# Checking the adjacency chunks on VectorE plane by plane in a two-layer graph kernel

## The chip, the cores and the metric

The kernel runs on 1 core of one Trainium2 chip. The metric is the device time of one execution in microseconds (us), as a median of runs.

## The reference

Two graph layers with a norm ahead of each, on 4096 nodes of 128 features; `adj` is 4096 x 4096 float32 (64 MiB), drawn as zeros and ones with few ones.

```
h = relu(layernorm(x))
Wh = h @ W0;  e = leaky_relu(Wh @ a[:128] + (Wh @ a[128:]).T, 0.2)
alpha = softmax(where((adj > 0) | eye, e, -9e15), axis=1)
x = x + alpha @ Wh
h = relu(layernorm(x))
msg = h @ W1 + B
weights = where(adj < 1, exp(-(1/adj - 1)**2 / 0.5), 0)
out = x + weights @ msg
```

For an `adj` that holds only zeros and ones the weights of the second layer are all zero. The kernel takes this short way, and has to make sure of it: every element of `adj` is checked while it passes, and only if one is neither zero nor one (or another limit is passed) does a general branch at the end compute everything anew. It is not taken with these inputs.

## The kernel before

The adjacency matrix comes in 32 chunks of 2 MiB. Chunk i is [128 partitions x 4096 elements]: four planes (HK = 4) of 1024 columns (CW), each plane another block of rows. It lies in a ring of six slots (`ring`, AR = 6). SP's queue issues `load_chunk(i)` for i from 6 on once chunk i-6 has been packed by TensorE, turned where a turn is due, and checked, by VectorE or by ScalarE (lines 357 to 368).

What happens to each chunk:
- TensorE's `pack(i)` (L538) adds eight rows of the matrix, as bits, into words in PSUM (two chunks a step, 16 steps, two chunks for each of 4 column blocks in each of 4 groups of rows).
- VectorE's `scan(step)` (L1022) takes the highest eight words of each segment (MAX8, L1032), `pick(n)` (L1035) the highest of all of a piece (5 pieces of steps), TensorE's `place(n)` (L608) and VectorE's `decode(n)` (L1141) turn them into node numbers (`index`, L1155); what doesn't fit in a lane goes through `pick_shared` (L1067) and `decode_shared` (L1101) into `shared_index` (L1123).
- GpSimd fetches the rows of `node_table` that the numbers name, with one indirect DMA for each 128 numbers (L470, 76 of them, in groups for each piece). Its loop waits in order for `index_set` and `shared_index_set`.
- VectorE's `weigh(g)` (L1167) makes weights of the rows and spreads them (L1189 to L1200, L1206, L1218), TensorE's `scatter(g)` (L673, L669) adds them up, VectorE's `epilogue(s)` (L1266) ends a group of 1024 rows.
- The first block of columns goes another way: TensorE's `turn_columns(i)` (L519, L534) transposes it and VectorE's `column(i)` (L1242, L1253 and L1263) weighs it. Chunks with part of the diagonal are cleaned (`clean_diagonal`, L1013, L1018; chunk 6 in place, `clear_diagonal`, L1006, L1010).
- The check: 19 chunks by ScalarE in two passes (L845, L848), 13 by VectorE (`DVE_CHECKED` = 0, 1, 2, 4, 6, 10, 11, 14, 18, 20, 23, 25, 27) in `check(i)` (L994). One instruction (L1002) compares (x >= 1) with x over all 4096 elements of a partition and adds the differences to `bad_v[:, n]`; its results elsewhere go to a place that nobody reads (`trash_v`, the memory of `summed`). Near the end `judge()` (L1306, L1320) takes the maximum over `bad_v`.

The order of work on VectorE is written out by hand: checks 0 and 1 at L1346, then a loop over i from 2 to 31 (L1396 to L1431) in which each i has its cleaning, its check, its decoding, column(i - 1), scan, pick, weigh and epilogue as tables at the top of the file give them (L110 to L126); the check of chunk 25 comes at i = 26 (`LATE_CHECK`). TensorE's order is that of L714 to L747: for each i pack, turn, place, scatter. All engines wait on semaphores; `checked_v` counts the checks of VectorE. ScalarE and GpSimd have their own loops (L890, L457).

Of the kernel before, what the change touches and what calls it, by code (L numbers as in the profile page):

```python
# [5 lines left out]
N, D, P = 4096, 128, 128  # L6
# [5 lines left out]
CW = N // CC  # L12
HK = 4
CHUNKS = SG * CC * 2
AR = 6
# [91 lines left out]
NVC, NAC = len(DVE_CHECKED), len(ACT_CHECKED)  # L107
# [21 lines left out]
def gnn_program(nc, x, adj, w0, a0, w1, b1, out):  # L129
    fp32, bf16, fp8, i32, u32 = (mybir.dt.float32, mybir.dt.bfloat16, mybir.dt.float8e4, mybir.dt.int32,  # L130
                                 mybir.dt.uint32)
    ALU, ACT, AX = mybir.AluOpType, mybir.ActivationFunctionType, mybir.AxisListType
# [10 lines left out]
    with ctx:  # L143
        def sb(name, shape, dt=fp32):
            return ctx.enter_context(nc.sbuf_tensor(name, shape, dt))

        def sem(name):
            return ctx.enter_context(nc.semaphore(name))

        ring = sb("adj_ring", [P, AR, HK * CW])  # L150
# [73 lines left out]
        shared_on = sb("shared_on", [P, 2, KB, KB, HK])  # L224
        edge_w = sb("edge_w", [P, GE, KB])
        full = sb("full", [P, len(PIECES), 3])
        bad_v = sb("bad_v", [P, NVC])
        signs = sb("signs", [P, NAC])
        sizes = sb("sizes", [P, NAC])
        excess = sb("excess", [P, NAC])  # L230
# [22 lines left out]
        trash_v = summed[:, :, :].bitcast(fp8).rearrange("p k n -> p (k n)")[:, 0:HK * CW]  # L253
# [34 lines left out]
        def acc_of(t):  # L288
# [17 lines left out]
        checked_v, signed, checked_a, diag_cleared, diag_clean, packed, scanned = (  # L306
            sem(n) for n in ("checked_v", "signed", "checked_a", "diag_cleared", "diag_clean", "packed", "scanned"))
# [6 lines left out]
            sem(n) for n in ("picked", "removed", "full_seen", "placed_set", "words_done", "decode_step", "index_set", "bits_set",  # L314
                             "table_stored"))
        gathered = [sem(f"gathered{g}") for g in range(RING_GROUPS)]
        weight_step, spread_set, scattered, acc_read, epilogue_step, finished, stored = (
            sem(n) for n in ("weight_step", "spread_set", "scattered", "acc_read", "epilogue_step", "finished",
                             "stored"))
# [625 lines left out]
        def _(dve):  # L945
# [48 lines left out]
            def check(i):  # L994
                n = DVE_CHECKED.index(i)
                dve.wait_ge(adj_ready[i % AR], (i // AR + 1) * 16)
                done = sum(1 for at in EPILOGUE_AT if at < i)
                if done:
                    dve.wait_ge(finished, done)
                if n:  # L1000
                    dve.wait_ge(checked_v, n)
                nc.vector.scalar_tensor_tensor(trash_v, ring[:, i % AR, :], 1.0, ring[:, i % AR, :],  # L1002
                                               ALU.is_ge, ALU.not_equal,
                                               accum_out=bad_v[:, n:n + 1], saturate=False).then_inc(checked_v, 1)

            def clear_diagonal(i):  # L1006
                dve.wait_ge(checked_v, DVE_CHECKED.index(i) + 1)
# [338 lines left out]
            for i in range(2):  # L1346
                check(i)
# [48 lines left out]
            for i in range(2, CHUNKS):  # L1396
                if i in CLEANED:
                    clean_diagonal(i)
                if i in DVE_CHECKED and i != LATE_CHECK:
                    check(i)  # L1400
# [17 lines left out]
                if i == LATE_CHECK + 1:  # L1418
                    check(LATE_CHECK)
# [119 lines left out]
```

## Time and profile before

| | before |
|---|---|
| median of 3 runs | 231.09 us (230.5 to 231.35) |
| the profiled execution | 230.85 us |
| its span | 229.0 us |
| mean granted TensorE clock | 0.88 |
| busy: DVE, ACT, PE, POOL | 195.2, 178.3, 153.4, 124.8 us |
| L1002, 13 instructions | 57.4 us, 4419 ns each |
| L470, gathers by index, 48 | 75.4 us, 1572 ns each |
| L470, gathers by shared index, 28 | 34.3 us, 1225 ns each |
| DMA | 76.95 MB, mean 336 GB/s |

PE is TensorE, PEld its weight loads, DVE VectorE, ACT ScalarE, POOL GpSimd, SP the engine that issues the loads. The table by stretches gives the busy time of each engine in each stretch, with the number of instructions, then the granted clock of TensorE as a share of 2.4 GHz, the busy share of the 16 DMA engines (rounding of packets can take it over 1) and what they moved. A row of the timeline is start, duration, engine, line, operation, tile written and tiles read, shapes and count; in brackets stands how long the engine had been idle before it and what released it. An indirect DMA's row on POOL is the making of its descriptors, not the transfer.

### The profile page before, as it was taken

What the parts mean: (1) busy time and instruction counts of PE and PEld (TensorE: products, weight loads), DVE (VectorE), ACT (ScalarE), POOL (GpSimd) and SP (SyncE); (2) the same over time, 40 slices, a digit from 0 to 9 for tenths busy, and PEclk for the clock granted to TensorE, in tenths of its full rate; (3) what the DMA queues carried; (4) which work ended last, traced back from release to release, by engine and by line L of the source; (5) the groups of instructions that cost most, each with busy time, mean ns of one, the idle gap of its engine ahead of it and who ended that gap; (6) DMA issues with size and microseconds to landing.
All of it is one profiled execution on the core that took longest, in us unless ns stands there. A gap on an engine that the chain in (4) does not pass through costs nothing.

```text
span 229.0 us, 3107 instructions
## 1 busy us (share of the span) xinstructions
PE 153.4 (67%) x893; PEld 102.3 (45%) x906; DVE 195.2 (85%) x595; ACT 178.3 (78%) x166; POOL 124.8 (55%) x130
## 2 busy tenths in 40 slices
PE   0286789930976956798299865975982697908450
PEld 0285565410455634465166522653750264508340
DVE  7975999908999999997799799689999996998584
ACT  0799983999399999989998879979393989992000
POOL 0198004000001788888759787783588782777600
PEclk9999999995697995999889997799799589785996
DMA  5999999999999999999999999999999994122002
GB/s 158 364 411 410 406 409 409 419 425 406 411 408 407 402 398 391 398 397 401 390 387 399 400 395 397 404 388 399 405 386 400 402 390 181 29 45 98 20 3 97
DMA packets 22388, 76.95 MB, mean 336 GB/s; under 512 B 2643, under 2 KB 3255, under 8 KB 22368
## 3 DMA queue, kind: packets, MB, share of 16 engines
q1 hardware_dynamic: 18624, 70.26, 78.4%
q0 software_dynamic: 3040, 5.34, 6.9%
q10 hardware_dynamic: 704, 1.12, 1.3%
q8 instruction: 9, 0.15, 0.3%
q14 instruction: 11, 0.09, 0.1%
HBM read 74.52 MB, written 4.28 MB: 344 GB/s over the span
## 4 chain that ended last, share of the span: by engine, by line
DMA 30%; DVE 27%; PE 19%; issue 12%; ACT 8%; POOLq 1%; POOL 1%; DVEq 0%; SPq 0%
DMA adj_ring<-in_adj 29%; PE bank L567 9%; DVE summed L1002 6%; ACT spread L814 5%; DVE hub_w L1235 3%; DVE cand L1032 2%; PE bank L669 2%; ACT whe L828 2%; ACT gathered_rows L820 1%; DVE spread L1218 1%; PE bank L554 1%; POOL gathered_rows L470 1%; POOLq L143 1%; DVE stats L979 1%; DMA gathered_rows<-node_table,shared_index 1%
## 5 line engine op out<-in xcount | busy, mean ns | idle before, releaser
L470 POOL DMA_INDIRECT gathered_rows<-node_table,index x48 | 75.4, 1572 | 46.3 <-DVE index L1155 32.9
L845 ACT ACTIVATE trash_a<-adj_ring,below_one 128x4096 fp8e4<-128x4096 f32 x19 | 70.5, 3708 | 11.4 <-DMA adj_ring<-in_adj 10.0
L567 PE MATMUL bank<-adj_ring,pack_w 128*128 128x512 bf16 (+3 forms) x257 | 72.5, 411 | 3.8 <-DMA adj_ring<-in_adj 3.0
L848 ACT ACTIVATE trash_a<-adj_ring 128x4096 fp8e4<-128x4096 f32 x19 | 68.7, 3617 | 0.6
L1002 DVE SCALAR_TENSOR_TENSOR summed<-adj_ring 128x4096 fp8e4<-128x4096 f32 x13 | 57.4, 4419 | 10.2 <-issue 6.6
L567 PEld LDWEIGHTS bank<-adj_ring,pack_w 128*128 128x128 bf16 x262 | 26.8, 106 | 34.9 <-issue 12.0
L470 POOL DMA_INDIRECT gathered_rows<-node_table,shared_index x28 | 34.3, 1225 | 8.5 <-issue 8.2
L669 PE MATMUL bank<-gathered_rows,spread 128*128 128x129 f32 x176 | 24.1, 295 | 7.4 <-DVE spread L1218 4.5
L669 PEld LDWEIGHTS bank<-gathered_rows,spread 128*128 128x128 f32 x176 | 22.7, 208 | 9.0 <-issue 8.9
L1032 DVE MAX8 cand<-bank 128x8 f32<-128x120 f32 (+25 forms) x82 | 23.3, 351 | 0.5 <-PE bank L567 0.5
L554 PE MATMUL bank<-codes,code_w 128*128 128x512 bf16 x24 | 11.0, 459 | 16.8 <-issue 14.9
L603 PE MATMUL bank<-whe,hub_w 128*128 128x129 f32 x64 | 10.6, 321 | 5.5 <-DVE hub_w L1239 5.4
L814 ACT ACTIVATE spread<-x_sb,shift,rstd 128x128 f32<-128x128 f32 x32 | 13.2, 498 | 0.0
L554 PEld LDWEIGHTS bank<-codes,code_w 128*128 128x128 bf16 x32 | 3.5, 109 | 20.5 <-issue 17.0
L603 PEld LDWEIGHTS bank<-whe,hub_w 128*128 128x128 f32 x64 | 9.3, 224 | 7.4 <-DVE hub_w L1239 7.2
L502 PE MATMUL bank<-w_sb,gathered_rows 128*128 128x130 f32 x64 | 10.4, 313 | 1.4 <-ACT whe L828 1.3
L490 PE MATMUL bank<-ident,spread 128*128 128x128 f32 x32 | 6.5, 338 | 6.8 <-ACT spread L814 6.8
L502 PEld LDWEIGHTS bank<-w_sb,gathered_rows 128*128 128x128 f32 x64 | 9.3, 223 | 2.6 <-ACT gathered_rows L820 2.3
L836 ACT ACTIVATE hub_mask<-bank 128x512 fp8e4<-128x512 f32 x8 | 4.3, 591 | 7.4 <-PE bank L515 7.4
L534 PE MATMUL bank<-ident_bf,adj_ring 128*128 128x128 bf16 x31 | 3.3, 231 | 9.8 <-DVE col_w L1263 6.2
L1235 DVE TENSOR_SCALAR hub_w<-r_hub,whe 128x128 f32<-128x128 f32 x32 | 8.9, 355 | 0.0
L663 PE MATMUL bank<-hub_whe,col_w 128*128 128x129 f32 x48 | 8.7, 357 | 0.0
(168 smaller groups left out, 228.1 us busy)
## 6 DMA issues: line engine op xcount, KB each, us to landing
adj_ring<-in_adj SPq DMA_DIRECT2D x32, 2048.0 KB, 23.3
node_table<-whe POOLq DMA_DIRECT2D x4, 532.0 KB, 10.9
x_sb<-in_x SPq DMA_DIRECT2D x8, 256.0 KB, 6.4
out<-outb ACTq DMA_DIRECT2D x2, 512.0 KB, 7.5
gathered_rows<-node_table,index POOLq DMA_INDIRECT x48, 5.9
out<-outb SPq DMA_DIRECT2D x1, 512.0 KB, 2.7
gathered_rows<-node_table,shared_index POOLq DMA_INDIRECT x28, 5.4
out<-outb SPq DMA_DIRECT2D x2, 192.0 KB, 2.3
```

What stands on the lines that cost most here:

```text
L470: pool.indirect_dma_start(out=rows[:, g % RING_GROUPS * GE + t, :], out_offset=None, in_=table, in_offset=bass.IndirectOffsetOnAxis(ap=row ...
L502: last = nc.tensor.matmul(bank[6 + half][:, b * (D + 2):(b + 1) * (D + 2)], hT[:, nb * P:(nb + 1) * P], w0_sb[:, :], start=(b == 0), stop= ...
L554: nc.tensor.matmul(to[:, :], code_w[:, 2 * c + half, :], codes[:, :], start=True, stop=False, skip_group_check=True)
L567: last = nc.tensor.matmul(to[:, lo:hi], pack_w[:, k, :], ring_hi[:, i % AR, row_at + lo:row_at + hi], start=False, stop=(k == KB - 1), ski ...
L603: last = nc.tensor.matmul(bank[7][:, 0:E1], hub_w[:, m % 2, b, :], whe[:, 4 * HUB_ORDER[m] + b, ONE:ONE + E1], start=(m + b == 0), stop=(m ...
L669: return nc.tensor.matmul(acc_of(t), spread[:, g % 2, t * KB:(t + 1) * KB, :], rows[:, g % RING_GROUPS * GE + turn, ONE:ONE + E1], start=F ...
L814: last = nc.scalar.activation(hn_block(b), x_sb[:, b, :], ACT.Identity, bias=shift[:, b:b + 1], scale=rstd[:, b:b + 1])
L845: nc.scalar.activation(trash_a[:, :], ring[:, i % AR, :], ACT.Sign, bias=below_one[:, :], scale=-1.0, accum_out=signs[:, n:n + 1], saturat ...
L848: nc.scalar.activation(trash_a[:, :], ring[:, i % AR, :], ACT.Abs, accum_out=sizes[:, n:n + 1], saturate=False).then_inc(checked_a, 1)
L1002: nc.vector.scalar_tensor_tensor(trash_v, ring[:, i % AR, :], 1.0, ring[:, i % AR, :], ALU.is_ge, ALU.not_equal, accum_out=bad_v[:, n:n + ...
L1032: last = nc.vector.max(cand[:, at * 8:(at + 1) * 8], word_bank(step, half)[:, lo:hi])
L1235: last = nc.vector.tensor_scalar(hub_w[:, m % 2, b, :], r_hub[:, :], whe[:, nb, QA:QA + 1], whe[:, nb, AA:AA + 1], ALU.mult, ALU.max)
```

## The change

`check(i)` issues four instructions, one for each plane of 1024 elements, in place of one over 4096. Each has its own column of `bad_v`, which grows from 13 to 52. All four write the first 1024 bytes of `trash_v`, so each waits for the one before it, on a new semaphore `plane_checked`; the last one counts `checked_v`, as the one instruction did. `judge` is unchanged and reduces the larger `bad_v`.

```diff
-        bad_v = sb("bad_v", [P, NVC])
+        bad_v = sb("bad_v", [P, NVC * HK])
...
+        plane_checked = sem("plane_checked")
...
                 if n:
                     dve.wait_ge(checked_v, n)
-                nc.vector.scalar_tensor_tensor(trash_v, ring[:, i % AR, :], 1.0, ring[:, i % AR, :],
-                                               ALU.is_ge, ALU.not_equal,
-                                               accum_out=bad_v[:, n:n + 1], saturate=False).then_inc(checked_v, 1)
+                for k in range(HK):
+                    plane = ring[:, i % AR, k * CW:(k + 1) * CW]
+                    if k:
+                        dve.wait_ge(plane_checked, n * (HK - 1) + k)
+                    nc.vector.scalar_tensor_tensor(trash_v[:, 0:CW], plane, 1.0, plane, ALU.is_ge, ALU.not_equal,
+                                                   accum_out=bad_v[:, n * HK + k:n * HK + k + 1], saturate=False).then_inc(
+                                                       checked_v if k == HK - 1 else plane_checked, 1)
```

## Rows read from the trace of the kernel before

**Rows 1.** The table by stretches: us, busy (x) PE, PEld, DVE, ACT, POOL, PEclk, DMA, GB/s.

```profile
10.00:20.00 10.00, 7.79 (x40) 7.02 (x40) 6.23 (x46) 10.00 (x30) 8.98 (x14) 1.00 1.03 414
...
180.00:186.00 6.00, 6.00 (x28) 3.38 (x27) 5.93 (x23) 5.31 (x5) 4.48 (x6) 0.63 1.02 394
...
191.00:193.00 2.00, 2.00 (x16) 1.01 (x14) 0.10 (x2) 1.91 (x3) 0.00 (x0) 1.00 0.38 147
```

**Rows 2.** Timeline of VectorE, its waits for transfers from 100 to 160 us.

```profile
110.08 0.23 DVE L1189 TENSOR_TENSOR edge_w<-r_slots,gathered_rows 128x64 f32<-128x64 f32 x1 [2.54 <-DMA gathered_rows<-node_table,index]
...
130.51 4.43 DVE L1002 SCALAR_TENSOR_TENSOR summed<-adj_ring 128x4096 fp8e4<-128x4096 f32 x1 [1.26 <-DMA adj_ring<-in_adj]
...
148.43 4.42 DVE L1002 SCALAR_TENSOR_TENSOR summed<-adj_ring 128x4096 fp8e4<-128x4096 f32 x1 [2.23 <-DMA adj_ring<-in_adj]
...
153.97 0.69 DVE L1018 TENSOR_TENSOR clean<-adj_ring,offdiag 128x512 bf16<-128x512 f32 x1 [1.11 <-DMA adj_ring<-in_adj]
```

**Rows 3.** Timeline of VectorE from 168 us.

```profile
168.11 4.42 DVE L1002 SCALAR_TENSOR_TENSOR summed<-adj_ring 128x4096 fp8e4<-128x4096 f32 x1
...
172.46 1.35 DVE L1032 MAX8 cand<-bank 128x8 f32<-128x376 f32 x3
173.73 4.43 DVE L1002 SCALAR_TENSOR_TENSOR summed<-adj_ring 128x4096 fp8e4<-128x4096 f32 x1
...
178.93 0.69 DVE L1263 TENSOR_TENSOR col_w<-col_w,bank 128x512 f32<-128x512 f32 x1
...
193.31 0.17 DVE L1155 SCALAR_TENSOR_TENSOR index<-words_i,empty_i 128x8 int32<-128x8 int32 x1
...
207.70 0.16 DVE L1123 TENSOR_TENSOR shared_index<-shared_column,shared_empty 128x4 int32<-128x4 int32 x1
```

**Rows 4.** Timeline of TensorE from 179 us.

```profile
179.68 0.61 PE L534 MATMUL bank<-ident_bf,adj_ring 128*128 128x128 bf16 x4 [6.23 <-DVE col_w L1263]
...
180.51 1.91 PE L567 MATMUL bank<-adj_ring,pack_w 128*128 128x512 bf16 x4
...
192.26 0.42 PE L622 MATMUL bank<-slots,own_lane 128*32 128x8 f32 x8
```

**Rows 5.** Timeline of GpSimd, its last 16 gathers.

```profile
194.24 0.99 POOL L470 DMA_INDIRECT gathered_rows<-node_table,index  x1 [4.15 <-DVE index L1155]
...
211.61 1.00 POOL L470 DMA_INDIRECT gathered_rows<-node_table,shared_index  x1 [0.30 <-issue]
```

**Rows 6.** Timeline of VectorE, checks of chunks 0, 1 and 6.

```profile
20.54 4.42 DVE L1002 SCALAR_TENSOR_TENSOR summed<-adj_ring 128x4096 fp8e4<-128x4096 f32 x1
...
25.07 4.43 DVE L1002 SCALAR_TENSOR_TENSOR summed<-adj_ring 128x4096 fp8e4<-128x4096 f32 x1
...
52.47 4.43 DVE L1002 SCALAR_TENSOR_TENSOR summed<-adj_ring 128x4096 fp8e4<-128x4096 f32 x1 [6.58 <-issue]
...
56.93 0.69 DVE L1010 TENSOR_TENSOR adj_ring<-adj_ring,offdiag 128x512 f32<-128x512 f32 x1
```

**Rows 7.** Timeline of VectorE, shorter instructions and the check of chunk 14.

```profile
99.19 1.23 DVE L1200 TENSOR_TENSOR spread<-edge_w,lane_of_p 128x1024 f32<-128x1024 f32 x1
100.33 4.42 DVE L1002 SCALAR_TENSOR_TENSOR summed<-adj_ring 128x4096 fp8e4<-128x4096 f32 x1
...
160.40 0.69 DVE L1018 TENSOR_TENSOR clean<-adj_ring,offdiag 128x512 bf16<-128x512 f32 x1
```

**Rows 8.** The answer on the tile adj_ring, its last line.

```profile
DMA to landing us min/median/max: 11.5/23.3/27.6
```

**Rows 9.** Timeline of GpSimd, gathers from 99 to 169 us.

```profile
99.68 1.61 POOL L470 DMA_INDIRECT gathered_rows<-node_table,index  x1 [0.30 <-issue]
...
148.04 0.99 POOL L470 DMA_INDIRECT gathered_rows<-node_table,shared_index  x1 [0.30 <-issue]
...
155.84 1.00 POOL L470 DMA_INDIRECT gathered_rows<-node_table,shared_index  x1 [0.30 <-issue]
...
168.79 4.61 POOL L470 DMA_INDIRECT gathered_rows<-node_table,index  x1 [0.31 <-issue]
```

## The prediction

> **What bounds the kernel now.** I read the table by stretches first. From 10 us to 186 us the DMA engines are busy for the whole time (a share of 1.02 or 1.03 in each of 18 stretches; the first and the last are shown) and move some 400 GB/s. At 191 us, when the last chunk of the adjacency matrix is nearly in, the share falls to 0.38 [rows 1]. So up to about 190 us no engine shortens the kernel by being quick: a chunk arrives when its bytes have been moved. VectorE (DVE) shows it: its checks of chunks 20 and 23 and the cleaning of chunk 24 start after waits for the DMA of 1.26, 2.23 and 1.11 us [rows 2].
>
> Then I read VectorE after the last of these waits, because from there nothing is given back. It cleans chunk 24 at 153.97 us [rows 2] and works without an idle time over 0.23 us to column(26) at 178.93, with the checks of chunk 25 (168.11) and chunk 27 (173.73) on the way [rows 3]. TensorE (PE) stands for 6.23 us until 179.68, released by that L1263, and from there works through packs 28, 29 and 30 without a pause to place(3) at 192.26 [rows 4]. VectorE makes the index of L1155 from it at 193.31 [rows 3], and GpSimd (POOL), idle for 4.15 us until then, issues its last 16 gathers from 194.24, one every 1.3 us or more, with no longer pause than 0.3 us; the last four start at 211.61 [rows 5]. They end at about 216.5, and VectorE's last weights and the epilogue follow.
>
> The chain of waits goes another way into the tail: through the load of chunk 31 and the shared index of L1123. I don't follow it. That index is ready at 207.86 [rows 3], but the first gather that needs it starts at 211.61, behind twelve others and with only its usual 0.30 us of idle time [rows 5]; that branch is over 3 us early. What sets the end is chunk 24, then VectorE to 179.6, TensorE to 193.0, VectorE to 193.5, GpSimd to 216.5.
>
> **The cost of one check.** An instruction of 4096 elements takes 4.42 us [rows 3]. L1018 with 512 elements takes 0.69 us and L1200 with 1024 takes 1.23 [rows 7], a slope of 0.54 / 512 = 1.05 ns an element; from L1200 to the check it is 3.19 / 3072 = 1.04. So a plane of 1024 takes 4.42 - 3072 x 0.00104 = 1.22 us, as L1200 does. From the start of a check to the start of what follows without a wait are 4.35 us (168.11 to 172.46) [rows 3], so the last plane costs 4.35 - 3.20 = 1.15. The three that are waited for cost more. Check 1, which waits for check 0, starts 4.53 us after it, and L1010, which also waits for its check, comes 4.46 us after it [rows 6]; less 3.20 that is 1.26 to 1.33. A check in four parts takes 3 x (1.26 to 1.33) + 1.15 = 4.93 to 5.14 us, that is 0.58 to 0.79 more. I take 0.70, nearer to check 1, which is the same kind of instruction behind its like. All 13 checks make VectorE 9.1 us busier.
>
> The Trainium skill ("VectorE: DVE Perf Modes", section "The DRAIN you can't avoid") says that a semaphore between two instructions costs nothing extra. By that the planes would be 1.15 us apart and a check would take 0.25 us more; rows 6, where the waiting instruction comes 0.11 and 0.18 us later than 4.35, don't agree, and the rows decide.
>
> **Which of the 13 count.** Checks 0, 1, 2 and 4 lie ahead of an idle time of 6.58 us before check 6 [rows 6]. They delay the first packs by some 1.2 us, while chunks are queued. Checks 6, 10, 11 and 14 lie ahead of the wait of 2.54 us for a gather at 110.08: 4 x 0.70 = 2.8 us, so 0.3 is left. Check 18 lies ahead of 1.26 us, check 20 ahead of 2.23, check 23 ahead of 1.11 [rows 2]; each covers the 0.70 before it, the first also the 0.3. What runs late in between are packs, and through them and the checks SP's next load_chunk. A chunk lands 11.5 us or more after its issue [rows 8] and 2 MB take 5.2 us at 400 GB/s, so at least 6 us of other transfers are ahead of it, and a load issued up to 2.8 us later lands no later. If that cover were gone it would be up to 0.70 at each. Two checks, 25 and 27, have no cover: 2 x 0.70 = 1.40 us (bounds 1.16 and 1.58) on the path to 179.68 and on to the index.
>
> **GpSimd.** A gather takes 1.00 us undisturbed. The one at 168.79, in the check of chunk 25, takes 4.61 and ends at 173.40, 0.87 us after the check (172.53). The one at 99.68 takes 1.61 and ends at 101.29, 0.87 after L1200 (100.42) [rows 3, 7, 9]. Eight of the 76 gathers, of 4.02 to 4.82 us, stand like this in eight checks, 3.3 us each over 1.00. What lets one go is the end of a single instruction: that of 99.68 got through although the check of 100.33 had already begun. So with planes a gather waits 1.2 us at most; by its beat of 1.3 us about two are held in a check, for 0.6 + 1.2 us. GpSimd gains 3.3 - 1.8 = 1.5 us a check, some 12 us. None of it reaches the end: it stands 4.15 us for the index before 194.24, and no check is left behind that. The Trainium skill says in "SBUF — State Buffer", section "Who interferes with whom", that a VectorE instruction with two SBUF inputs shuts out a GpSimd one that reads SBUF for the whole instruction; the trace agrees, with these 0.87 us.
>
> What earlier gathers cost is DMA time. Four start from 148.04 to 155.84 [rows 9], most of whose bytes move behind chunk 24. By the 4.5 us gained in checks 18, 20 and 23 one to four of them go ahead of it, each 128 x 133 x 4 bytes = 68 KB, 0.17 us at 400 GB/s. Chunk 24 lands 0 to 0.7 us later; I take 0.2, as of those that move forward part was ahead before.
>
> **The rest.** judge reduces 52 partial results in place of 13: 39 x 1.05 ns = 0.04 us, nothing even on the path. Nothing is added to SP's or ACT's queue.
>
> The sum on the profiled execution: 230.85 + 1.40 + 0.20 = 232.45 us. That execution (span 229.0 us, 1.85 around it) lies 0.24 under the median of the runs, so the forecast is 231.09 + 1.60 = **232.7 us**, 0.7% more. Its own range is 232.0 to 233.4 (both ends of the two terms: 1.16 and 2.28, the lower less 0.25 for the runs' scatter).
>
> **Rivals.** (1) The delay is partly covered by TensorE's clock. After its 6.23 us of standing TensorE runs at 1.2 GHz for a while: the granted clock is 0.63 from 180 to 186 us, and four matmuls of L567 take 1.91 us [rows 1, 4]. If the clock comes back at the same moment although TensorE starts 1.6 us later, half of that is made up: 231.9, or 231.8 with no shift of chunk 24. Nothing in one trace ties the return to TensorE's start, which is for it; it can as well fall the other way, which is against it.
> (2) The gathers count after all, and the kernel gets faster. The place is the wait of 2.54 us at 110.08 [rows 2]: gathers come there some 5 us earlier. If the loads behind it had been late because of it, 2.5 us come off, less 1.40 for the uncovered checks: 230.0. It decides only if the DMA has gaps before 190 us; shares of 1.02 and more [rows 1] speak against it.
> (3) Planes and gathers hold each other up. If a gather that has got in between two planes makes the next plane wait until it is done, it costs up to 0.87 us; two a check in checks 25 and 27 are 3.5 us: 236.2. The Trainium skill, same page and section, has it that issue order decides who blocks. Against it speaks the check at 100.33, which took 4.42 us like the others with a gather under way until 101.29 [rows 7, 9].
> (4) The planes cost less than rows 6 say: 0.25 us a check gives 231.09 + 0.5 + 0.2 = 231.8.
>
> **How the numbers follow.** Forecast 0.54; (1) 0.20; (4) 0.10; (2) 0.08; (3) 0.08. The low end, 231.0, takes in (1) and (4) with the scatter of the runs and no shift; the high end, 234.0, the upper bounds (233.4) and a weak form of (3), one gather in each check. What is left out is (2), most of (3) and small tails. A measurement of this kernel tells about 0.5%, 1.2 us here, from no change, so the line is at 232.25. (1), (4) and a little of the forecast's lower side lie under it: same 0.35, slower 0.57, faster 0.08.
>
> **What would show it.** Right: 52 instructions on VectorE of about 1.22 us, 1.26 to 1.33 apart within a check; no gather over 2.3 us in a check; the cleaning of chunk 24 at 154.0 to 154.7; TensorE's wait ahead of turn_columns(27) ending near 181.3; the index of piece 3 near 195; GpSimd's last gather ending near 218. Wrong: that index still at 193.5 (a cover that I missed); planes over 1.4 us apart (rival 3); planes 1.15 apart (4); DMA shares clearly under 1.0 before 190 us.

## The result and the profile after

| | before | after |
|---|---|---|
| median | 231.01 us (230.5 to 231.35, 4 runs) | 233.91 us (232.61 to 234.35, 4 runs) |
| the profiled execution, its span | 230.85, 229.0 us | 234.35, 232.1 us |
| mean granted TensorE clock | 0.88 | 0.852 |

The ratio is 1.0118, with a 95% interval of 1.0074 to 1.0163: the change costs 2.7 us (1.7 to 3.8), where 1.6 had been forecast. Line numbers of after: the check is L1007 (before L1002), `clean_diagonal` L1023, `index` L1160, `column` L1268, `shared_index` L1128, the gathers L471.

The page of after, its groups (busy us, mean ns of one | idle before them, and what ended it):

```profile
L471 POOL DMA_INDIRECT gathered_rows<-node_table,index x48 | 52.1, 1085 | 73.0 <-DVE index L1160 59.5
...
L1007 DVE SCALAR_TENSOR_TENSOR summed<-adj_ring 128x1024 fp8e4<-128x1024 f32 x52 | 63.8, 1227 | 8.6 <-issue 3.8
...
L471 POOL DMA_INDIRECT gathered_rows<-node_table,shared_index x28 | 32.2, 1150 | 8.5 <-issue 8.2
```

Thirteen checks of 4419 ns have become 52 planes of 1227 ns, 6.4 us more work on VectorE. The 76 gathers take 84.3 us in place of 109.7. GpSimd has gained 25.4 us, and the kernel is slower all the same: what GpSimd gained shows up as its idle time ahead of the index.

The timeline of VectorE after (start, duration, operation; in brackets the idle time before it and what released it), from the checks of chunks 20, 23, 25 and 27 to its last epilogue:

```profile
130.76 1.23 DVE L1007 SCALAR_TENSOR_TENSOR summed<-adj_ring 128x1024 fp8e4<-128x1024 f32 x1 [0.61 <-DMA adj_ring<-in_adj]
...
149.82 1.23 DVE L1007 SCALAR_TENSOR_TENSOR summed<-adj_ring 128x1024 fp8e4<-128x1024 f32 x1 [2.73 <-DMA adj_ring<-in_adj]
...
155.02 0.69 DVE L1023 TENSOR_TENSOR clean<-adj_ring,offdiag 128x512 bf16<-128x512 f32 x1 [0.16 <-DMA adj_ring<-in_adj]
...
168.98 1.22 DVE L1007 SCALAR_TENSOR_TENSOR summed<-adj_ring 128x1024 fp8e4<-128x1024 f32 x1
170.12 0.08 DVE L1007 DVE_READ_ACCUMULATOR summed<-adj_ring 128x1 f32 x1
170.24 1.23 DVE L1007 SCALAR_TENSOR_TENSOR summed<-adj_ring 128x1024 fp8e4<-128x1024 f32 x1
...
171.51 1.23 DVE L1007 SCALAR_TENSOR_TENSOR summed<-adj_ring 128x1024 fp8e4<-128x1024 f32 x1
...
172.78 1.23 DVE L1007 SCALAR_TENSOR_TENSOR summed<-adj_ring 128x1024 fp8e4<-128x1024 f32 x1
...
175.20 1.21 DVE L1007 SCALAR_TENSOR_TENSOR summed<-adj_ring 128x1024 fp8e4<-128x1024 f32 x1
...
180.98 0.69 DVE L1268 TENSOR_TENSOR col_w<-col_w,bank 128x512 f32<-128x512 f32 x1
...
195.63 0.17 DVE L1160 SCALAR_TENSOR_TENSOR index<-words_i,empty_i 128x8 int32<-128x8 int32 x1
...
229.21 0.61 DVE L1307 SCALAR_TENSOR_TENSOR outb<-summed,rden,x_sb 128x128 f32<-128x128 f32 x2
```

TensorE and GpSimd after, same columns:

```profile
181.73 0.61 PE L535 MATMUL bank<-ident_bf,adj_ring 128*128 128x128 bf16 x4 [8.48 <-DVE col_w L1268]
...
194.58 0.42 PE L623 MATMUL bank<-slots,own_lane 128*32 128x8 f32 x8
...
219.36 6.49 PE L670 MATMUL bank<-gathered_rows,spread 128*128 128x129 f32 x32 [3.44 <-DVE spread L1223]
```

```profile
169.66 1.41 POOL L471 DMA_INDIRECT gathered_rows<-node_table,index  x1 [0.30 <-issue]
171.37 1.00 POOL L471 DMA_INDIRECT gathered_rows<-node_table,index  x1 [0.30 <-issue]
172.68 1.00 POOL L471 DMA_INDIRECT gathered_rows<-node_table,index  x1 [0.30 <-issue]
...
196.57 1.00 POOL L471 DMA_INDIRECT gathered_rows<-node_table,index  x1 [11.46 <-DVE index L1160]
...
218.00 1.07 POOL L471 DMA_INDIRECT gathered_rows<-node_table,shared_index  x1 [0.30 <-issue]
```

Followed through, against the rows of before:
- The cleaning of chunk 24 is at 155.02, 1.05 later [rows 2]. Not all of this is the transfer of chunk 24. VectorE's check of chunk 23 already starts 1.39 us later, as chunk 23 lands (149.82 against 148.43), and takes 0.60 more; VectorE is free only at 154.86, 0.89 after the moment at which it started the cleaning before. The wait of 1.11 us ahead of the cleaning is down to 0.16.
- The check of chunk 25 starts 0.87 later, column(26) 2.05 later [rows 3]: the two checks between them brought 1.18, that is 0.59 each.
- TensorE's wait ends 2.05 later, place(3) is 2.32 later [rows 4], the index and the first gather 2.32 and 2.33 [rows 3, 5]. The last gather ends at 219.07 (218.00 + 1.07), 2.6 us later.
- VectorE's last epilogue ends at 229.82 (229.21 + 0.61); before it ended at 226.14: 3.7 later. About 1.1 us have been added behind the last gather. After that the end of the kernel gives 0.6 back; the span is 3.1 longer.

What was added behind the gathers comes with a lower clock of TensorE. Its last two scatters are one row of 6.49 us after, with no pause in it (above); before they were two rows:

```profile
216.58 2.02 PE L669 MATMUL bank<-gathered_rows,spread 128*128 128x129 f32 x16 [3.28 <-DVE spread L1218]
219.84 2.02 PE L669 MATMUL bank<-gathered_rows,spread 128*128 128x129 f32 x16 [1.23 <-DVE spread L1218]
```

The table by stretches (us, busy and count of PE, PEld, DVE, ACT, POOL, granted clock, DMA share, GB/s), first after, then before:

```profile
177.00:187.00 10.00, 5.27 (x17) 2.66 (x18) 9.83 (x27) 7.51 (x4) 6.28 (x7) 0.51 1.03 388
...
218.00:225.00 7.00, 5.64 (x26) 5.67 (x27) 4.29 (x21) 0.00 (x0) 1.07 (x1) 0.51 0.04 7
```

```profile
177.00:187.00 10.00, 7.32 (x34) 4.24 (x35) 9.79 (x31) 9.31 (x5) 8.01 (x7) 0.66 1.02 393
...
218.00:225.00 7.00, 2.63 (x22) 2.28 (x20) 6.62 (x28) 0.00 (x0) 0.00 (x0) 1.00 0.09 32
```

From 177 to 187 us the clock is at its lower level, 1.2 GHz, for longer than before, after a wait of TensorE of 8.48 us; from 218 to 225 us, where the last scatters run, it is at 1.2 in place of 2.4 GHz.

### The profile page after: what moved, and what is told of

It reads as the page before. It is cut to its first block, busy times and chain, and to the rows that moved or that the text cites. A ratio compares the mean times of both kernels' runs of the same rounds, so it can differ in the third digit from the quotient of the medians.

```text
span 232.1 us, 3198 instructions
## 1 busy us (share of the span) xinstructions
PE 157.6 (68%) x906; PEld 106.1 (46%) x906; DVE 202.4 (87%) x673; ACT 178.5 (77%) x166; POOL 100.6 (43%) x130
## 4 chain that ended last, share of the span: by engine, by line
DMA 28%; DVE 25%; ACT 21%; PE 12%; issue 11%; DVEq 0%; POOL 0%; SPq 0%; ACTq 0%; POOLq 0%
DMA adj_ring<-in_adj 26%; ACT trash_a L846 10%; DVE summed L1007 8%; ACT trash_a L849 7%; PE bank L568 5%; PE bank L670 4%; ACT spread L815 3%; DMA gathered_rows<-node_table,shared_index 2%; DVE spread L1223 1%; PE bank L555 1%; DVE cand L1037 1%; DVE stats L980 1%; PE bank L664 1%; DVE summed L1278 1%; DVE summed L1299 1%
## 5 line engine op out<-in xcount | busy, mean ns | idle before, releaser
L471 POOL DMA_INDIRECT gathered_rows<-node_table,index x48 | 52.1, 1085 | 73.0 <-DVE index L1160 59.5
L568 PE MATMUL bank<-adj_ring,pack_w 128*128 128x512 bf16 (+3 forms) x262 | 71.8, 404 | 0.6 <-DMA adj_ring<-in_adj 0.6
L1007 DVE SCALAR_TENSOR_TENSOR summed<-adj_ring 128x1024 fp8e4<-128x1024 f32 x52 | 63.8, 1227 | 8.6 <-issue 3.8
L568 PEld LDWEIGHTS bank<-adj_ring,pack_w 128*128 128x128 bf16 x262 | 26.6, 105 | 31.2 <-issue 9.6
L471 POOL DMA_INDIRECT gathered_rows<-node_table,shared_index x28 | 32.2, 1150 | 8.5 <-issue 8.2
L670 PE MATMUL bank<-gathered_rows,spread 128*128 128x129 f32 x176 | 26.2, 313 | 8.2 <-DVE spread L1211 3.7
L670 PEld LDWEIGHTS bank<-gathered_rows,spread 128*128 128x128 f32 x176 | 24.8, 225 | 9.6 <-issue 9.1
L555 PE MATMUL bank<-codes,code_w 128*128 128x512 bf16 x32 | 14.3, 447 | 14.2 <-issue 12.1
L535 PEld LDWEIGHTS bank<-ident_bf,adj_ring 128*128 128x128 bf16 x31 | 2.2, 106 | 18.5 <-DVE col_w L1268 10.2
```

The costliest lines, as they stand in the source:

```text
L471: pool.indirect_dma_start(out=rows[:, g % RING_GROUPS * GE + t, :], out_offset=None, in_=table, in_offset=bass.IndirectOffsetOnAxis(ap=row ...
L555: nc.tensor.matmul(to[:, :], code_w[:, 2 * c + half, :], codes[:, :], start=True, stop=False, skip_group_check=True)
L568: last = nc.tensor.matmul(to[:, lo:hi], pack_w[:, k, :], ring_hi[:, i % AR, row_at + lo:row_at + hi], start=False, stop=(k == KB - 1), ski ...
L670: return nc.tensor.matmul(acc_of(t), spread[:, g % 2, t * KB:(t + 1) * KB, :], rows[:, g % RING_GROUPS * GE + turn, ONE:ONE + E1], start=F ...
L1007: nc.vector.scalar_tensor_tensor(trash_v[:, 0:CW], plane, 1.0, plane, ALU.is_ge, ALU.not_equal, accum_out=bad_v[:, n * HK + k:n * HK + k + ...
```

## The experiments

One table first, since most verdicts are read from it: starts of the cleaning of chunk 24 (L1018), column(26) (L1263) and index 3 (L1155), and the end of the last gather, each from one profiled execution; then the ratio of the runs. Lines by before's numbers. "Planes" says which checks are split.

| kernel | planes | clean 24 | column(26) | index 3 | last gather ends | ratio (95%) |
|---|---|---|---|---|---|---|
| before | none | 153.97 | 178.93 | 193.31 | 216.5 | 1 |
| e0_before_again | none | 154.48 | 179.67 | 194.19 | 216.9 | one run, 232.15 us |
| after | all 13 | 155.02 | 180.98 | 195.63 | 219.1 | 1.0118 (1.0074 to 1.0163) |
| e1_two_whole | all but 25, 27 | 155.75 | 180.54 | 195.17 | 218.1 | 1.0014 (0.9992 to 1.0035) |
| e2_only_two | 25, 27 | 153.74 | 180.10 | 194.52 | 216.9 | 1.0031 (1.0 to 1.0061) |
| e3_no_wait | all 13, unchained | 156.07 | 181.31 | 196.03 | 219.3 | 1.006 (1.0027 to 1.0092) |
| e6_pad | none, 11 lengthened | 153.87 | 178.65 | 193.17 | 216.2 | 1.0029 (1.0003 to 1.0056) |
| e7_half_gathers | none | 152.84 | 178.76 | 193.14 | 215.9 | one run, 230.42 us |
| e8_split_18_20_23 | 18, 20, 23 | 155.06 | 179.85 | 194.46 | 217.7 | one run, 232.84 us |

**The kernel before once more**, for how far two profiles of one kernel lie apart.

> The kernel before, once more, for a second trace. If the later cleaning of chunk 24 after the change (155.02 us against 153.97) is an effect of the change, it stands at 153.7 to 154.3 here. If it is scatter between executions, it can lie anywhere from 153.5 to 155. Time 230.5 to 231.4 us.

Chunk 24 is cleaned 0.5 us later and index 3 comes 0.9 later than in the first profile, with not a line changed. So shifts of half a us at chunk 24 are no evidence by themselves. The executions here with whole checks ahead of chunk 24 and all gathers (these two, e2, e6 and the five kernels with check 27 moved, below: nine in all) have it at 153.6 to 154.5.

**The covered checks split, the two uncovered ones whole**, and the reverse.

```diff
+PARTS = [1 if i in (25, 27) else HK for i in DVE_CHECKED]     # e1_two_whole
+PARTS = [HK if i in (25, 27) else 1 for i in DVE_CHECKED]     # e2_only_two
...
-                for k in range(HK):
+                for k in range(PARTS[n]):
```

> Four planes for all checks but those of chunks 25 and 27, which stay one instruction. My theory (only these two have no cover; the rest costs through chunk 24 alone, which lands later as gathers move ahead of it): no gather over 2.3 us in the eleven split checks, chunk 24 cleaned at 154.5 to 155.1, TensorE's long wait for column 26 ends at 180.2 to 180.9, time 231.4 to 232.2 us. Rival A (every check's 0.6 us counts in part, VectorE being 87% busy): 233 us or more, as with all 13. Rival B (chunk 24's delay was scatter): 230.9 to 231.3 us.

> Four planes for the checks of chunks 25 and 27 alone. My theory: chunk 24 cleaned at 153.7 to 154.3, eight gathers become six of 4 us or more, TensorE's long wait ends at 180.8 to 181.1 (1.2 later than before), and the clock of TensorE may add up to 1 us behind it: time 232.2 to 233.2 us. Rival A: 2/13 of the whole, 231.4 us or less. Rival C (the early gathers themselves cause the delay, not the length of the checks): 231.0 to 231.4 us.

e2 is the clean one. Chunk 24 stays where it was (153.74), VectorE's check of chunk 25 starts at 168.10 [rows 3: 168.11], and column(26) comes at 180.10 in place of 178.93, index 3 at 194.52 in place of 193.31: 1.17 and 1.21 us for two checks. The two checks behind the last wait cost what their planes cost and hand it on in full; the runs give 0.7 us (0 to 1.4). Of the 1.2 us part is won back in the tail: the last gather ends only 0.4 us later, as one gather there was held 0.2 us where 1.0 had been usual.

e1 shows a second thing. No check between 155 and 181 us is longer than before, and yet column(26) is 1.61 later, all of it since chunk 24 is cleaned at 155.75 (154.5 to 155.1 had been expected). But its profiled execution, 233.28 us, is 1.3 above the median of its own runs, 232.01, and the runs say 0.3 us (-0.2 to 0.8). So that delay is real in the profile, and over the runs it is worth 0.8 us at most.

**What delays chunk 24?** Longer checks, or gathers that go earlier? Three kernels: whole checks, each of the eleven covered ones followed by 0.6 us of useless reduction; ten of the 20 gathers of three groups left out, so that fewer packets run ahead of chunk 24; planes in 18, 20 and 23 alone.

```diff
+                if i not in (25, 27):                                     # e6_pad
+                    nc.vector.tensor_reduce(padded[:, n:n + 1], x_sb[:, 0:4, :].rearrange("p b d -> p (b d)"), AX.X,
+                                            ALU.max).then_inc(pad_done, 1)
...
+ISSUED = [rows // 2 if g in (3, 4, 5) else rows for g, rows in enumerate(ROWS_OF_GROUP)]    # e7_half_gathers
...
+PARTS = [HK if i in (18, 20, 23) else 1 for i in DVE_CHECKED]             # e8_split_18_20_23
```

> The kernel before, whole checks, with a reduction of 512 elements (0.6 us, one SBUF input) behind each check but those of chunks 25 and 27: the eleven covered checks get longer by what the planes cost, but the gathers stay held. Theory (waits cover this; chunk 24 came late through the gathers): chunk 24 cleaned at 153.7 to 154.6, eight gathers over 2.3 us, time 231.0 to 231.7 us like before. Rival E (chunk 24 came late because longer checks release ring slots late): cleaned at 155 or later, 232.0 us or more.

> The kernel before without half of the gathers of groups 3, 4 and 5 (10 of 20 left out, so those rows of the result are not computed rightly). It measures what one gather costs the DMA ahead of chunk 24. By the 0.17 us of its bytes, the price in my prediction, chunk 24 is cleaned 1.2 to 1.7 us earlier (those of them that were ahead of it), at 152.3 to 152.8. If small pieces cost more, 0.25 us each as the rates of 80 to 90 us and 130 to 140 us suggest, at 151.2 to 152.2.

> Four planes for the checks of chunks 18, 20 and 23 alone, between which and chunk 24 the gathers of groups 3 to 5 run. Theory (gathers ahead of chunk 24): the last gather of group 5 starts near 147 in place of 155.8 and chunk 24 is cleaned at 154.7 to 155.7. Rival (the delay builds up from the early checks on): 153.9 to 154.4.

VectorE in e6, e7 and e8, from three timelines:

```profile
153.87 0.69 DVE L1023 TENSOR_TENSOR clean<-adj_ring,offdiag 128x512 bf16<-128x512 f32 x1 [1.03 <-DMA adj_ring<-in_adj]
```

```profile
152.84 0.69 DVE L1019 TENSOR_TENSOR clean<-adj_ring,offdiag 128x512 bf16<-128x512 f32 x1 [0.62 <-DMA adj_ring<-in_adj]
```

```profile
150.11 1.23 DVE L1011 SCALAR_TENSOR_TENSOR summed<-adj_ring 128x1024 fp8e4<-128x1024 f32 x1 [2.05 <-DMA adj_ring<-in_adj]
...
155.06 0.69 DVE L1027 TENSOR_TENSOR clean<-adj_ring,offdiag 128x512 bf16<-128x512 f32 x1
```

With the checks longer but whole, chunk 24 is where it was: eleven checks with 0.6 us behind each are covered (the runs' 0.7 us, interval 0.1 to 1.3, I can't place). With fewer gathers it comes 1.1 to 1.6 us earlier. With three checks split, it comes some 1.1 late. As longer checks alone (e6) don't do it, the gathers that planes let go early are what is left. Late issues of the loads aren't it either: in e6 SP's issue of the load of chunk 24 ends 2.2 us later than in before (128.99 against 126.78), and the chunk lands as before. In before, four of them start from 148.04 to 155.84 [rows 9]; in after GpSimd, ahead of its work, has started its last four by 146.34:

```profile
142.31 1.04 POOL L471 DMA_INDIRECT gathered_rows<-node_table,shared_index  x1 [0.31 <-issue]
143.65 1.00 POOL L471 DMA_INDIRECT gathered_rows<-node_table,shared_index  x1 [0.30 <-issue]
144.95 1.08 POOL L471 DMA_INDIRECT gathered_rows<-node_table,shared_index  x1 [0.30 <-issue]
146.34 1.00 POOL L471 DMA_INDIRECT gathered_rows<-node_table,shared_index  x1 [0.30 <-issue]
```

The delay is there a chunk earlier. The check of chunk 23, released by the landing, starts at 147.8 to 149.1 in the ten executions with whole checks (e7 among them) and at 149.8 to 150.9 in the four with planes. With 0.6 us more in it, VectorE then comes hardly before chunk 24 itself: the cleaning waits 0.16 us in after and e1, 0.53 in e3 and not at all in e8.

By their bytes four gathers cost 0.7 us at most. Chunk 24's packets go through 16 DMA engines, and the trace has the moment when each is done. In the five kernels with whole checks that I read (before, e0, e2, e4, e6) the median engine is done at 151.9 to 152.4 us and the last at 153.7 to 154.5; in the four split ones (after, e1, e3, e8) at 152.4 to 152.6 and 154.9 to 156.0. The median moves by 0.4 us, as the bytes would have it; the last engine of the 16 falls another us behind, and the cleaning waits for the last. Why just one falls back I haven't found, and no price for one gather follows: in four of the nine executions above the four gathers start from 147.9 to 148.2 on, in the other five from 153.6 or later, and chunk 24 is cleaned at 153.9 to 154.0 and at 153.6 to 154.5. Nor is what is won at chunk 24 handed on: in e7 it is 1.13 us, and 0.17 at column(26), as VectorE then waits 0.58 us for TensorE ahead of 166.60.

**Planes without the chain.** All 13 checks in planes, each plane with its own quarter of `trash_v`, so that only the check before has to be done, not the plane before.

```diff
                 if n:
+                    dve.wait_ge(plane_checked, n * (HK - 1))
                     dve.wait_ge(checked_v, n)
                 for k in range(HK):
...
-                    if k:
-                        dve.wait_ge(plane_checked, n * (HK - 1) + k)
-                    nc.vector.scalar_tensor_tensor(trash_v[:, 0:CW], plane, ...
+                    nc.vector.scalar_tensor_tensor(trash_v[:, k * CW:(k + 1) * CW], plane, ...
```

> All 13 checks in four planes as in the changed kernel, but each plane writes its own quarter of trash_v, so that none waits for the one before it (only the next check waits for all). My theory: planes 1.15 us apart in place of 1.27, a check 4.60 us long, 0.35 us shorter each, so the two uncovered checks give back 0.7 us: 233.2 us. Gathers: the end of one instruction lets a gather go even where the next follows at once, so none takes over 2.3 us in a check. Rival D (it is the pause at the semaphore that lets a gather in): gathers of 4 us or more are back in the checks.

```profile
170.03 1.22 DVE L1006 SCALAR_TENSOR_TENSOR summed<-adj_ring 128x1024 fp8e4<-128x1024 f32 x1
171.18 0.08 DVE L1006 DVE_READ_ACCUMULATOR summed<-adj_ring 128x1 f32 x1
171.18 1.22 DVE L1006 SCALAR_TENSOR_TENSOR summed<-adj_ring 128x1024 fp8e4<-128x1024 f32 x1
...
172.32 1.22 DVE L1006 SCALAR_TENSOR_TENSOR summed<-adj_ring 128x1024 fp8e4<-128x1024 f32 x1
...
173.47 1.22 DVE L1006 SCALAR_TENSOR_TENSOR summed<-adj_ring 128x1024 fp8e4<-128x1024 f32 x1
```

The planes are 1.15 us apart where nothing is waited for, 1.265 where each waits for the one before it: the wait costs 0.12 us, and 0.35 of the 0.60 us of a check are the three waits. The rows show what is waited for: a plane's sum is read out in a row of its own (DVE_READ_ACCUMULATOR, 0.08 us). The next plane starts together with it where nothing is waited for (171.18), and 0.12 us after its start where there is a wait (170.12, 170.24 in after). There is no gap left between planes, but gathers still get in: none takes over 2.3 us, eleven take 1.94 to 1.99, and all 76 take 93.8. So what lets one in is the end of an instruction, not a gap. The kernel costs 1.4 us (0.6 to 2.1) against before. That is less than after, though the two intervals overlap.

**Check 27 moved off VectorE's path**, whole, to i = 31 behind `pick_shared(3)`; or ahead of `decode(3)`, where VectorE stands. Two waits follow the new place: check 27 waits for two epilogues, and the epilogue at `s == 1` for one check less.

```diff
-                if i in DVE_CHECKED and i != LATE_CHECK:
+                if i in DVE_CHECKED and i not in (LATE_CHECK, 27):
...
+                if i == 31:
+                    check(27)
```

> The kernel before, whole checks, with the check of chunk 27 moved from ahead of column(26) to i = 31, behind decode(3) and pick_shared(3) (no load waits for it). If the check of chunk 27 is on the path, as I say, all 4.35 us of it leave the stretch ahead of TensorE's wait: that wait ends at about 175.3, the path is then held by the landing of chunk 30 at 187.9 (pack 30, 2.1 us), index 3 comes at 191 to 192 in place of 193.3, and the time is 229.0 to 230.3 us. Rival (the path goes through chunk 31 and index 4, as the chain of waits has it): nothing gained, 231 us, or lost, as the scan of chunk 31 comes behind the moved check.

> Whole checks as in the kernel before; check 27 alone is moved, from its place ahead of column(26) to VectorE's standing ahead of decode of piece 3. With check 27 moved behind that decode, TensorE's wait ended at 175.7 in place of 179.6, but pack 30 then stood for the landing of chunk 30 (189.6) and one gather of the tail was held for 5.10 us. Here no gather stands under the check and the landing still holds pack 30. Theory (index 3 is bound by whichever of VectorE and the landing is later, and a whole check costs where a gather stands under it): check 27 fills about 188 to 192.5, the index is ready near 193, the gathers end near 216, 230.3 to 231.3 us, 3.5 or more under the other place. Rival (the place of check 27 alone cost, the held gather did not matter): 233.5 or more.

e4 lies 4.6 us above the range expected of it: the ratio is 1.0168 (1.0129 to 1.0206), 234.87 us. TensorE and GpSimd of e4:

```profile
175.73 0.40 PE L534 MATMUL bank<-ident_bf,adj_ring 128*128 128x128 bf16 x4 [1.85 <-DVE col_w L1263]
...
189.60 0.39 PE L554 MATMUL bank<-codes,code_w 128*128 128x512 bf16 x1 [2.70 <-DMA adj_ring<-in_adj]
...
191.94 0.42 PE L622 MATMUL bank<-slots,own_lane 128*32 128x8 f32 x8
```

```profile
193.93 1.00 POOL L470 DMA_INDIRECT gathered_rows<-node_table,index  x1 [6.48 <-DVE index L1155]
195.23 5.10 POOL L470 DMA_INDIRECT gathered_rows<-node_table,index  x1 [0.30 <-issue]
```

Check 27 was on the path: without it TensorE's wait ends at 175.73, 3.95 us earlier [rows 4]. But only 0.3 us of that reaches the index (192.99), since pack 30 now stands for the landing of chunk 30 at 189.60 (187.9 had been expected): once VectorE is 4 us quicker, the transfer is the later of the two. And the moved check, 4.40 us from 194.70, shuts out the second gather of GpSimd's last 16 for 5.10 us, where nothing gives it back: the last gather ends at 219.96. In e5, with the check where no gather stands, the second gather takes 1.20 us, the last one ends at 215.12, and the runs are level with before (ratio 0.9995, 0.9962 to 1.0028), some 4 us under e4. This agrees with the held gather as what e4 lost; it isn't the 0.3 us or more under before that I expected.

**Do planes pay where GpSimd is what the end waits for?** Four planes for check 27 alone in e4's place (e9). Then the same with `place(3)` ahead of `pack(30)` on TensorE, which frees the index from chunk 30 (e10), and that with the check whole (e11).

```diff
             for i in range(CHUNKS):
+                if i == 30:
+                    place(PICK_AT[i])
                 pack(i)
...
-                if i in PICK_AT:
+                if i in PICK_AT and i != 30:
                     place(PICK_AT[i])
```

> As the kernel with check 27 behind the decode of piece 3 (234.87 us, gathers ending at 219.96), but this one check in four planes; all others whole. Theory (planes free the gather under a check, and that counts where GpSimd is what the end waits for): the gather of 5.10 us becomes at most 2.3, the gathers end 2 to 3.5 us earlier, 231.5 to 233 us, 2 us or more under that kernel. Rival (planes are only a cost of 0.6 us; VectorE's own work in the tail sets the end): 234.9 to 235.5.

> As the run with check 27 in planes behind the decode of piece 3, and TensorE does place(3) ahead of pack(30), so that the index of piece 3 no longer waits for the landing of chunk 30. Theory: place(3) near 188, index 3 near 189.5, the gathers start near 190.5 and end near 213.5 to 214.5 (the last four wait for the shared index after chunk 31), 228.0 to 230.0 us, under both kernels. Rival (the end goes by the last chunks' landing and TensorE's packs, not by index 3): 231 or more, although the index is 3 us earlier.

> As the run with place(3) ahead of pack(30), but check 27 whole. Theory (a whole check holds the gather under it on GpSimd's tail): one gather of 4 to 5 us in the tail, the gathers end 2 to 3.5 us later than with planes, 1.5 to 3 us above that run. Rival (the last gathers wait for the shared index of chunk 31 anyway, so a held gather ahead of it is covered): within 0.7 us of it.

| | gather under the check | index 3 | last gather ends | median | ratio (95%) |
|---|---|---|---|---|---|
| e4, whole | 5.10 us | 192.99 | 219.96 | 234.87 us | 1.0168 (1.0129 to 1.0206) |
| e9, planes | 1.55 us | 194.68 | 220.88 | 234.69 us | 1.0117 (1.0084 to 1.015) |
| e11, early place, whole | 5.09 us | 188.44 | 215.87 | 231.95 us | 0.9984 (0.9947 to 1.0021) |
| e10, early place, planes | 1.54 us | 188.26 | 213.80 | 229.8 us | 0.9889 (0.983 to 0.9947) |

GpSimd in e10, then in e11:

```profile
190.50 1.54 POOL L472 DMA_INDIRECT gathered_rows<-node_table,index  x1 [0.30 <-issue]
...
208.55 0.99 POOL L472 DMA_INDIRECT gathered_rows<-node_table,shared_index  x1 [2.25 <-DVE shared_index L1134]
```

```profile
190.68 5.09 POOL L470 DMA_INDIRECT gathered_rows<-node_table,index  x1 [0.30 <-issue]
```

Here the same edit has the other sign. Planes free 3.55 us of GpSimd's time on its last stretch; the last four gathers then wait 2.25 us for the shared index, which follows chunk 31, and 2.07 us remain at the last gather; the runs say 2.2 us (e11 less e10: 0.0095; by the two intervals together about 0.6 to 3.8). e10 beats both kernels: 2.6 us (1.2 to 3.9) under before. In e9 the gather is freed as well, but its last four gathers wait 3.00 us for the shared index; 1.2 us come out by the ratios (about 0 to 2.4), where 2 or more were expected, and its median of 234.69 lies nearer to its rival (234.9 or more) than to 231.5 to 233. Its profile had index 3 a further 1.7 us late, with TensorE's clock low at pack 30, so profile and runs can't be set side by side there.

## Why the prediction came out as it did

Right: the kernel is slower, through VectorE's last checks, TensorE's wait, the index and GpSimd's gathers, and the time lies in the range. The size was 1.2 us short of the median.

- **A plane, and a check in four.** 1.22 us was said, 1.22 to 1.23 measured. The distance, 1.265, is at the low end of 1.26 to 1.33, so a check costs 0.60 and not 0.70. I had leaned on check 1 behind check 0 as its own kind; the other row, L1010 behind check 6 [rows 6], was the nearer. In after each plane waits, and they are 1.265 apart; in e3 they don't wait, and are 1.15 apart. The Trainium skill ("VectorE: DVE Perf Modes", section "The DRAIN you can't avoid") has a semaphore between two instructions for nothing; these two distances don't agree with it for an instruction that also writes its sum.
- **Two of 13 count.** Shown by e2: 1.17 us to column(26), 1.21 to the index (1.40 forecast), and by e6, in which the other eleven are longer and chunk 24 stays in its place. The covers ahead of chunk 23 were where they were said to be: the waits before checks 20 and 23 are now 0.61 and 2.73 us, and the wait for a gather at 110.08 is gone: the row at 110.26 has none. The last one, "check 23 ahead of 1.11", didn't hold with planes: chunk 23 lands 1.39 late, check 23 takes 0.60 more, and VectorE is free 0.89 after the moment at which the cleaning started before. With the longer checks of e6, in which chunk 23 isn't late, it held.
- **Chunk 24 later by the gathers.** The mechanism is right (e7, e8); the size failed, 0.20 of 0 to 0.7 against 1.05 in after's profile and 1.1 or more in e1, e3 and e8. That these kernels also have chunk 23 late, which the prediction didn't look at, is part of it. Two steps under the term fell short. "One to four of them go ahead": all four did. And bytes over 400 GB/s is what the median of the 16 engines shows, 0.4 us; the chunk is there when the last of them is, another us on. What it weighs over the runs, in which e1 costs only 0.3 us, is less than the profiles show.
- **GpSimd's gain.** 12 us were forecast, 25.4 came. The step that failed is "about two are held in a check, for 0.6 + 1.2 us". After one held gather (169.66, 1.41 us) the next start at 171.37 and 172.68, 1.30 apart, 0.14 and 0.10 us ahead of a plane, and aren't held: planes 1.265 apart and gathers 1.30 apart fall into step. That this gain doesn't reach the end was right: the idle time before the index grew from 4.15 [rows 5] to 11.46 us.
- **The clock.** Rival 1 had half the delay made up by it. It went the other way: four matmuls of L568 still take 1.91 us, and index 3 is 2.32 late where TensorE's start was 2.05 late. And a term that I didn't have: behind the last gather TensorE ran at 1.2 GHz, 1.1 us. Whether this is tied to the change isn't shown. From the end of the last gather to the end of VectorE's last instruction 10.75 us pass in after, e1 and e8, 11.0 in e10 and 12.4 in e5, and 9.6 to 9.8 in all others; e3 has all planes and the latest gathers of the first table, and has the short tail. That is three of the four kernels with planes ahead of chunk 24, and two of the ten others. In the five with the long tail the last two scatters follow each other without a pause (5.45 to 6.74 us in one row), in the others with one. TensorE stood for 3.44 us ahead of them in after and for 3.28 in before, where its clock stayed at 2.4 GHz; what sets it I leave open.
- **The other rivals.** (2): the wait of 2.54 us did go, and nothing came of it, as the DMA had no gap. (3): in the checks of chunks 10 and 14 planes that start together with a gather are 1.26 long and 1.30 apart; the other checks of after don't show it. That is 0.04 us a plane at most. (4) needs planes without waits.

```profile
103.70 1.26 DVE L1007 SCALAR_TENSOR_TENSOR summed<-adj_ring 128x1024 fp8e4<-128x1024 f32 x1
...
105.00 1.26 DVE L1007 SCALAR_TENSOR_TENSOR summed<-adj_ring 128x1024 fp8e4<-128x1024 f32 x1
...
106.31 1.26 DVE L1007 SCALAR_TENSOR_TENSOR summed<-adj_ring 128x1024 fp8e4<-128x1024 f32 x1
```

The sum that the profile of after gives: 1.18 (two checks) + 0.87 (chunks 23 and 24, as far as it reaches check 25) + 0.27 (clock up to the index) + 0.24 (GpSimd's last stretch) + 1.1 (clock behind it) - 0.6 (end) = 3.1 us, its span's growth. The runs of after say 2.7, those of e1 and e2 together 1.0 (0.3 + 0.7). The intervals (1.7 to 3.8, and about 0.1 to 1.9) just overlap; how much of after's cost is chunk 24 and the clock, and how much the scatter of four runs, stays open. The two checks are the part that is shown twice.

## What to carry to other kernels

Splitting a long VectorE instruction like this check, with two SBUF inputs, cost VectorE 0.25 us for the three more instructions, 0.60 where they wait for each other, and gave GpSimd back nearly all of the time for which its gathers were held. So do it only where a gather of the path that sets the end stands under the instruction (e10 against e11), and leave it where GpSimd's next pause is for something else: the page showed that here as idle time of the gathers <- index. Before moving a long instruction off one engine's path, look at what stands beside it in its new place (e4), and at which transfer comes due next.

## What the runs showed of the hardware

- A gather that is being made gets in at the end of any single VectorE instruction, even if the next has begun already (e3: planes without a gap, and no gather over 2.3 us, against 5.10 under a whole check in e4). The Trainium skill ("SBUF — State Buffer", section "Who interferes with whom") gives the holder the shared pair for the whole instruction; the runs agree, and show that the lock is not kept from one instruction to the next.
- Waiting for one's own engine's previous instruction, one with an accumulated sum, costs 0.12 us on VectorE (1.265 against 1.15 us), from the start of the row that reads out the sum.
- A chunk spread over 16 DMA engines is late by its last engine: in the four kernels with planes, which put up to four gathers of 68 KB each ahead of it, the median engine is 0.4 us later than in five with whole checks, and the last 1 us more. That the gathers do it is concluded from e6, e7 and e8; how isn't known.
